# Layer 0's sums two steps at a time, tables before the images, attention's first loads in seven parts, and the last convolution on VectorE alone

## The reference, cut to what matters

```python
p2 = x[:, :, _I2] * x[:, :, _J2]                       # all pairs of a group
y2 = einsum('bgihw,goi->bgohw', p2, W2) + b2
p3 = x[:, :, _I3] * x[:, :, _J3] * x[:, :, _K3]        # all triples
y3 = einsum('bgihw,goi->bgohw', p3, W3) + b3
l = x + y2 * beta2 + y3 * beta3 * 0.1
```

```python
g = clip(bn(conv1x1(l, w_inside)), 0, 6)
f = softmax(softmax(theta.T @ theta, axis=keys), axis=queries)   # theta = l[:, :32]
out = g @ f                                            # 3136 x 3136 per image
out = bn(depthwise3x3(out, w_dw)) + l
```

## Time and profile before

| what | us |
|---|---|
| runs | 5437.07, 5438.80, 5445.94 |
| median | 5438.8 |
| profiled execution, its own time | 5436.95 |
| its span, first to last instruction | 5435.1 |
| PE busy | 5268.8 (97%) |
| ACT busy | 5133.4 (94%) |
| DVE busy | 4469.9 (82%) |
| POOL busy | 4464.1 (82%) |
| layer 0, until its last sums | 0 to 771 |
| attention and the last image | 771 to 5435 |

### The profile page before, as it was taken

One profiled execution on the slowest core, in us unless ns is written; L12 is line 12 of the kernel. 1 busy time (PEld: TensorE's weight loads), 2 busy tenths in 40 slices (PEclk: granted clock), 3 DMA queues, 4 the chain that ended last, 5 costly groups with the idle time before them and its releaser, 6 DMA issues. The chain is left out here.

```text
span 5435.1 us, 91114 instructions
## 1 busy us (share of the span) xinstructions
PE 5268.8 (97%) x33426; PEld 2665.2 (49%) x33426; DVE 4469.9 (82%) x8979; ACT 5133.4 (94%) x3028; POOL 4464.1 (82%) x1872
## 2 busy tenths in 40 slices
PE   7989999999999999999999999999999999999997
PEld 3434444555555555455545455555555555555453
DVE  7878887888888888888888888888888888888887
ACT  6878889999999999999999999999999999999996
POOL 5666655888888898988888898888888989888888
PEclk9999989999999999999999999999999999999998
DMA  6877861222222222222222222222222222222220
GB/s 134 170 164 161 164 117 35 53 55 61 52 52 61 61 61 61 61 61 60 56 60 54 60 49 55 57 58 59 53 55 58 61 61 61 61 61 61 60 44 13
DMA packets 226760, 380.05 MB, mean 70 GB/s; under 512 B 158037, under 2 KB 175246, under 8 KB 216078
## 3 DMA queue, kind: packets, MB, share of 16 engines
q1 hardware_dynamic: 225136, 373.85, 32.9%
q10 hardware_dynamic: 1182, 0.37, 0.0%
HBM read 258.49 MB, written 102.74 MB: 66 GB/s over the span
## 5 line engine op out<-in xcount | busy, mean ns | idle before, releaser
L945 DVE TENSOR_SCALAR_CACHE_REDUCE at_ring<-at_S 128x1176 f32<-128x1176 f32 (+1 forms) x2352 | 2889.5, 1242 | 425.5 <-PE at_S L1065 394.6
L826 POOL TENSOR_TENSOR at_ZP<-at_ZP,at_ring 128x1568 f32<-128x1568 f32 x640 | 2274.1, 3586 | 293.2 <-ACT at_ring L894 276.7
L888 ACT ACTIVATE at_ring<-at_ring,at_NM 128x3136 f32<-128x3136 f32 x784 | 2278.5, 2906 | 109.8 <-DVE at_NM L954 100.0
L1096 PE MATMUL at_AV<-at_ring,at_GT 128*64 128x392 f32 x12800 | 2325.2, 504 | 39.3 <-issue 33.3
L894 ACT ACTIVATE at_ring<-at_ring,at_RZ 128x3136 f32<-128x3136 f32 x784 | 2273.3, 2900 | 0.0
L1065 PE MATMUL at_S<-at_THM,at_THS 128*128 128x392 f32 x6144 | 1460.0, 365 | 49.5 <-DVE at_ring L945 44.9
L1096 PEld LDWEIGHTS at_AV<-at_ring,at_GT 128*64 128x64 f32 x12800 | 861.4, 138 | 1152.4 <-issue 1084.4
L1065 PEld LDWEIGHTS at_S<-at_THM,at_THS 128*128 128x128 f32 x6144 | 1029.7, 189 | 719.6 <-DVE at_ring L945 492.6
L839 POOL TENSOR_TENSOR at_OUTB<-at_OUTB,at_ZB 128x1568 f32<-128x1568 f32 x248 | 883.5, 3563 | 16.9
L1102 PE MATMUL at_AV<-at_ring,at_ones 128*32 128x392 f32 x7168 | 663.8, 497 | 0.0
L466 DVE TENSOR_TENSOR l_U<-l_TY,l_XB 128x448 f32<-128x448 f32 x896 | 497.1, 617 | 110.0 <-PE l_TY L505 109.8
(11 more groups left out here) (80 smaller groups left out, 2496.0 us busy)
## 6 DMA issues: line engine op xcount, KB each, us to landing
l_X<-in_x SPq DMA_DIRECT2D x128, 392.0 KB, 7.3
at_THM<-hld SPq DMA_DIRECT2D x128, 392.0 KB, 6.5
at_THS<-hld SPq DMA_DIRECT2D x256, 192.0 KB, 3.9
at_CIN<-att SPq DMA_DIRECT2D x62, 406.0 KB, 7.2
at_ZB<-rzd SPq DMA_DIRECT2D x62, 406.0 KB, 5.3
yd<-l_YO SPq DMA_DIRECT2D x128, 196.0 KB, 6.1
att<-at_ACC SPq DMA_DIRECT2D x248, 98.0 KB
at_OUTB<-yd SPq DMA_DIRECT2D x62, 392.0 KB, 8.1
```

The source lines that it names most:

```text
L826: e.tensor_tensor(z, z, v, ALU.add).then_inc(g_add, 1)
L888: e.activation(v, v, ACT.Exp, bias=NM[:, i:i + 1], accum_out=ZS[:, i:i + 1]).then_inc(a_p1, 1)
L945: e.tensor_scalar(ring[:, s % RING, QC * a_:QC * b].rearrange("p (b w) -> p b w", w=QC), PS[:, k % 2, 0:b - a_, 0:QC], 1.0, None, ALU.mult ...
L1096: ins = e.matmul(dst[64 * j:64 * j + 64, 0:QC], GT[fl.n % 2][:, keys_of(fl.n, t), :], ring[:, slot, q:q + QC], start=(i == 0), stop=(i == ...
```

## The change

- **Sums in pairs.** After the selects of each even step u >= 2, PE runs `sums(u-2)` and `sums(u-1)`, and none in odd steps; DVE's two closes follow each other too. `t_use` and `y_use` are numbered to match.
- **Start.** The first 448 columns of image 0 are loaded alone (`s_l0`), then the tables, then the rest of image 0 and images 1 to 3. Three memsets go from DVE to POOL.
- **Early loads** go out in seven parts, after images 8, 10, ..., 20.
- **Split.** POOL's `split(n)` stands after step 7n + 14 (`SPLIT_AT`).
- **Last image.** POOL has no part in it. DVE does rows 0 to 13 of both halves, then rows 14 to 27, and SP stores each part. The bias and the zeroed borders (`last_prepare`) stand ahead of the last z evacuations, and the two reciprocals one and three evacuations later than before.

```diff
@@ layer0
     def t_use(u, j):
-        return 4 * u + j + max(0, u - 1)
+        return 4 * u + j + 2 * max(0, (u - 1) // 2)
     def y_use(u):
-        return 4 * min(u + 2, NU) + u
+        return 4 * min(u - u % 2 + 3, NU) + u
...
-        load(0)
+        for b in range(4):
+            c = 32 * (b // 2)
+            e.dma_start(X2[0][32 * b:32 * b + 32, 0:CH], x[0, c:c + 32, 0:CH]).then_inc(s_l0, 16)
...
-        for n in range(1, min(NX, n_img)):
+        for n in range(min(NX, n_img)):
             load(n)
...
-            if n == min(EARLY, n_img - 1):
-                for i in range(min(2, n_img - 1)):
+            if EARLY <= n < EARLY + 2 * len(early) and (n - EARLY) % 2 == 0:
+                for i in range(2):
                     e.wait_ge(s_st[i], 64)
                     e.wait_ge(s_hl[i], 128)
-                early()
+                early[(n - EARLY) // 2]()
...
-            n, r = divmod(u - 12, NCH)
+            n, r = divmod(u - SPLIT_AT, NCH)
...
-            if u >= 1:
+            if u >= 2 and u % 2 == 0:
+                close(u - 2)
                 close(u - 1)
+        close(NU - 2)
         close(NU - 1)
...
-            if u >= 1:
+            if u >= 2 and u % 2 == 0:
+                sums(u - 2)
                 sums(u - 1)
+        sums(NU - 2)
         sums(NU - 1)
@@ build, sync
+            early = [lambda: first_keys(0), lambda: first_keys(1), lambda: ths(0, 0), lambda: ths(0, 1),
+                     shared_keys, lambda: first_y(0), lambda: first_y(1)]
@@ build, vector
-                O3 = OUTL.rearrange("p (r w) -> p r w", w=W)[:, 0:SHARE, :]
...
+                for part in range(2):
+                    r = 14 * part
+                    O3 = OUTL.rearrange("p (r w) -> p r w", w=W)[:, r:r + 14, :]
+                    for k_, v in enumerate(CENTRE_FIRST):
...
-            for i in range(2):
-                end = dve_order.index(("ev", index["z", last, len(groups(last, n_img)) - 1, i])) + 1
-                dve_order.insert(end, ("rl", i))
+            dve_order.insert(dve_order.index(("ev", index["z", last, len(groups(last, n_img)) - 1, 0])), ("lp",))
+            g = len(groups(last, n_img)) - 1
+            dve_order.insert(dve_order.index(("ev", index["z", last, g, 1])) + 1, ("rl", 0))
+            dve_order.insert(dve_order.index(("ev", index["o", last, g, 1])) + 1, ("rl", 1))
```

More of the change, by code:

```diff
@@ L411, in gpsimd @@
             parts(u)
-            n, r = divmod(u - 12, NCH)
+            n, r = divmod(u - SPLIT_AT, NCH)
             if r == 0 and n >= 0:
                 split(n)
-        for n in range(max(0, (NU - 1 - 12) // NCH + 1), n_img):
+        for n in range(max(0, (NU - 1 - SPLIT_AT) // NCH + 1), n_img):
             split(n)
@@ L735, in last_out @@
                 e.dma_start(CINL[0:64, 29, 1:57], CINL[64:128, 1, 1:57]).then_inc(s_halo, 16)
-                for done, r0, r1 in ((v_fin, 0, SHARE), (g_fin, SHARE, 28)):
-                    e.wait_ge(done, 1)
+                for part in range(2):
+                    e.wait_ge(v_fin, part + 1)
                     for h in range(2):
-                        e.dma_start(out[last, :, HW // 2 * h + W * r0:HW // 2 * h + W * r1],
-                                    OUTL[64 * h:64 * h + 64, W * r0:W * r1]).then_inc(s_out, 16)
+                        lo = HW // 4 * part
+                        e.dma_start(out[last, :, HW // 2 * h + lo:HW // 2 * h + lo + HW // 4],
+                                    OUTL[64 * h:64 * h + 64, lo:lo + HW // 4]).then_inc(s_out, 16)
             todo = []
@@ L764, in _, with first_keys, shared_keys, first_y @@
                     todo.append((r + 8, last_in, ()))
-            def early():
+            def first_keys(h):
+                for blk in range(2 * h, 2 * h + 2):
+                    e.dma_start(THM[0][32 * blk:32 * blk + 32, :].bitcast(F32), hld[0, blk % 2]).then_inc(s_thm[0], 16)
+            def shared_keys():
                 e.wait_ge(g_ms, 7)
[L768 to L771, removed]
+                for n in range(2):
                     thl(n)
-                e.wait_ge(v_ms, 3)
-                for b in range(4):
+            def first_y(h):
+                e.wait_ge(g_yt, 3)
+                for b in range(2 * h, 2 * h + 2):
                     yt(0, b)
+            early = [lambda: first_keys(0), lambda: first_keys(1), lambda: ths(0, 0), lambda: ths(0, 1),
+                     shared_keys, lambda: first_y(0), lambda: first_y(1)]
             l0_sync(e, early)
@@ L792, in _ @@
             e.memset(THL[:, :, :].bitcast(F32), 0.0).then_inc(g_ms, 1)
+            e.wait_ge(g_ms, 7)
+            for i in range(2):
+                e.memset(YT[i][64:65, :], 1.0).then_inc(g_yt, 1)
+                e.wait_ge(g_yt, i + 1)
+            e.memset(THM[1][64:65, 0:2 * 896].bitcast(F32), 1.0).then_inc(g_yt, 1)
+            e.wait_ge(g_yt, 3)
             l0_gpsimd(e)
@@ L988, in last_rows @@
                 e.wait_ge(v_ol, 1)
[L989 to L997 removed]
+                for part in range(2):
+                    r = 14 * part
+                    O3 = OUTL.rearrange("p (r w) -> p r w", w=W)[:, r:r + 14, :]
+                    for k_, v in enumerate(CENTRE_FIRST):
+                        i, j = divmod(v, 3)
+                        if k_ == 3:
+                            e.wait_ge(s_halo, 32)
+                        ins = e.scalar_tensor_tensor(out=O3, in0=CINL[:, r + i:r + i + 14, j:j + 56], scalar=w9[:, v:v + 1],
+                                                     in1=O3, op0=ALU.mult, op1=ALU.add)
+                        if k_ < 8:
+                            link(ins)
+                    ins.then_inc(v_fin, 1)
             def evacuate(f):
```

56 lines of the change are left out of this document (15 added, 41 removed).

## The result

| what | before | after |
|---|---|---|
| median of the runs | 5441.80 (4 runs) | 5413.59 (4 runs) |
| lowest, highest | 5437.07, 5445.94 | 5409.05, 5418.00 |
| profiled execution, its own time | 5436.95 | 5416.31 |
| its span | 5435.1 | 5414.5 |

The median before is over one run more than the 5438.8 that I forecast from (a run of 5444.80 was added). The ratio is 0.9948, with a 95% interval of 0.9931 to 0.9966: about 28 us faster (18 to 38); against 5438.8 it would be 25. I had forecast 5406.2, with a range of 5392 to 5419. The time lies in the range, 7.4 us above the forecast. Two terms of the sum were off by over 5 us, in opposite directions, and attention, which the change doesn't touch, took another length in the two profiled executions.

A forecast was written before the change was run, and what follows sets the result against it. PE was taken to bound layer 0 and ACT to fill attention. Pairs 1.0, stall 16.7, start 6.6 and tail 8.3 sum to 32.6 us off 5438.8, giving 5406.2; own range 5396 to 5416, overall 5392 to 5419.

The forecast's parts named there:

- Term 1: Layer 0, sums in pairs: waiting for ACT's copy takes back nearly all saved turns; 6.39 against 6.40 a pair, 1 us gained.
- All turns are saved: Rival, layer 0: ACT does not hold PE, a pair takes 6.05, 38 us more gained, 5368; chance 8%.
- ACT doesn't catch up: Rival, layer 0: ACT starts instructions 0.96 apart, a select comes about 0.1 us late, 11 us lost, 5417; chance 10%.
- DVE becomes the bound: Rival, layer 0: PE's second products wait for DVE's closes, a pair takes 7.1, 78 us lost, 5484; chance 4%.
- Term 2: Stall near 274 us in layer 0: early loads in parts and the later `split` remove it all, 16.7 us gained.
- the parts don't do what they say: Rival, stall: the four 784 KB parts each push `TH` by 3.8 us, 15 of 16.7 us return, 5421; chance 6%.
- Term 3: Kernel start: tables no longer wait behind six sevenths of image 0, 1.38 MB; 6.6 us gained.
- my signs: Listed trace signs of the forecast, among them PE's first matmul at 23.4 and eighteen DVE taps of 0.97 us.
- Term 4: Last image: DVE-only taps gain 7.8, the longer store loses 0.5, the reciprocals gain 1.0; 8.3 us gained in the tail.
- Attention at nothing: Attention, where ACT works 4505.6 of 4614 us: the change touches nothing there, 0 us.

The follow-up runs named there:

- experiment 3: Changed kernel with ACT copying only half the columns to `XB`, the rest a constant filled in at the start: 5399.88 us, ratio 0.9926, pairs of 6.34 us.
- experiment 4: Changed kernel with half the columns of ACT's copies and half of DVE's outer products left out: 5380.5 us in one run, pairs of 6.11 to 6.12 us.
- experiment 9: Kernel before with only the early loads in seven parts: 5419.57 us in one run.
- experiment 10: Kernel before with only `split` two steps later, the early loads still all at once: 5422.92 us in one run.
- experiment 7: Changed kernel with the first two sevenths of image 0 ahead of the tables instead of one: 5416.42 us in one run.
- experiments 1 and 8: Changed kernel with sums again one step at a time: 5391.84 us, ratio 0.9915; kernel before with the changed last image alone: 5430.55 us, ratio 0.9986.

## Why the prediction was right or wrong

- **The sign and most of the size were right.** 28 us by the medians and by layer 0 and tail, against 32.6 forecast. The result is in the forecast's own range of 5396 to 5416. That it came so near is in part luck: the pairs were 10.4 us worse than forecast, and the start's 5.3 and the stall's 1.3 us more than forecast made up for over half of it.
- **Term 1, the pairs: the mechanism was right, one size was off.** "Select 0 of the next step must wait until ACT has read select 1" is what the trace shows, at the place forecast, and with the waits in the other order a pair is 6.40, where I had 6.39. The step that failed is "0.05 later PE may go on": I took it from an instruction of ACT. It measured 0.114 on PE, since the late wait stood in an instruction of its own, and a further 0.03 to 0.05 was lost in the step behind it, where the two halves of each product run 0.03 apart. That is 0.084 a pair over the old 6.40, and 112 times that is 9.4 us lost where 1.0 was to be gained. My bound of 7 us for this term was too narrow; a number that is multiplied by 112 deserved its row from the same engine, with the same waits.
- **"All turns are saved" was a fair rival and wrong twice over.** ACT's copy held PE (experiment 3), and behind it DVE would have (experiment 4). 6.12 with both halved confirms the turns' price. The Trainium skill's sentence that changing the tiling mode drains TensorE (in "TensorEngine Tiling (Array Packing)", section Key Properties) agrees with that: 0.28 of the 0.35 a pair is there when nothing else waits.
- **"ACT doesn't catch up" didn't happen**: the odd select 0 follows the sums at once (506.04), and ACT has 1.13 us to spare by then. **"DVE becomes the bound"** didn't either, in the changed kernel; its second products come at 503.33, its outer products end at 503.05. But it is nearer than I thought, as experiment 3 shows.
- **Term 2, the stall: right.** 17.1 us of it and 0.9 of small ones, against 16.7. The rival "the parts don't do what they say" fell with experiment 9. What I read as cover, the two later steps, is worth 6.7 us by itself (experiment 10), and only clears the small stalls once the parts are there.
- **Term 3, the start: 6.6 forecast, 11.9 measured.** "At 207 GB/s that is 6.6 us", from the bytes ahead of the tables, should have been 9.4: the half table on ACT's queue landed 7.7 us after its issue, not after the 8.9 of its median before. My bound of 7.6 rested on that median, which was itself taken among the image's transfers. And "it is 7.1 us of DVE work, unchanged" was wrong: POOL had been working beside it, and no longer is. That is 3.3 us more (experiment 7). "Lands with the tables" was wrong too: the rest of image 0 came at 17.38, 3.9 us after them, and the first select lost 0.7 by it. PE's first matmul, due at 23.4 by my signs, came at 17.32.
- **Term 4, the tail: right in sum, by errors that cancel.** A tap is 1.035 us and starts every 1.06, not 0.97: 19.1 against 17.5, so the taps gain 6.2 and not 7.8. The spreading starts 0.3 earlier instead of 1.0 (my own rows gave 0.85), because the bias took 2.13 us (1.03 before) beside POOL's 4.10; in experiments 1 and 8, where it took 1.03, the spreading starts 1.4 earlier. Against that, the spreading ran at full clock (2.85 us at a granted 1.00, against 4.36 in the earlier trace rows at 0.65), which I hadn't counted, and gave 1.5. The longer store cost the 0.5 that I had.
- **Attention at nothing** was right as a term and wrong for one execution: its length differs by up to 14 us between executions, more than the error of any term.

## What to carry to other kernels

Give the wait that comes last the place where the engine passes it soonest: of two waits on one instruction the late one belongs on the instruction itself, which here meant first in the program, and in a loop of 112 rounds that was 9 us. When a turn or a switch is saved by batching, follow the buffers one round further, to what holds the engine next, before counting the gain: the plain kernel without pairs is 10 us faster in layer 0. And before a difference of 10 us is put down to an edit, compare the stretches that the edit doesn't touch.

## What the runs showed of the hardware that I had not expected

- A released weight load of PE starts 0.05 us after the releasing instruction's end if the wait stands on it, and 0.114 after if the wait has an instruction of its own ahead of it (502.102 to 502.152, and 501.944 to 502.058; the same in the median of 100 pairs of each kernel).
- DVE beside a busy POOL: 1.23 us instead of 0.43 for a product of 128x256, 0.97 instead of 0.16 for one of a single column, each ending 0.02 to 0.3 us after POOL's instruction. The taps of 1568 elements without POOL take 1.852, about what those of 1176 took beside it (16.62 for nine, 1.85).
- A small table behind other transfers on the queues, at the same size: 16.5 us from issue to landing with the whole of image 0 ahead of it, 7.7 with a seventh.
- Attention's length goes with the time at half clock, 82 to 119 us of it per execution, for a program whose instructions there are the same.
